# The prologue of a fused cross-attention kernel: x loaded before the context, queries in two 64-row halves, first keys written by ScalarE and VectorE

## The reference

```python
C_q  = layernorm(x) @ Wq_d                     # 512 -> 64
C_kv = ctx @ Wkv_d                             # 1601 rows, 512 -> 32
q    = (C_q @ W_qk).reshape(b, n, 16, 32)      # 16 heads
scores = einsum('bnhl,bkl->bhnk', q, C_kv) / sqrt(32)
x = x + einsum(softmax(scores), (C_kv @ Wv_u)) # by head
x = x + attention(layernorm(x), k_cache, v_cache, ...)
x = x + ffn(layernorm(x), w1, w2, w3, ...)
```

## Time and profile before

| | |
|---|---|
| Median of 3 runs | 947.01 us (943.29 to 948.63) |
| The profiled execution, its own time | 948.39 us |
| Its span in the trace | 946.6 us |
| TensorE busy | 889.5 us (94%) |
| VectorE, ScalarE, GpSimd busy | 64%, 55%, 44% |
| Mean granted clock of TensorE | 0.976 |
| First `scores` | 61.14 us |

### The profile page before, as it was taken

One profiled execution on the slowest core, in us unless ns is written; L12 is line 12 of the kernel. 1 busy time (PEld: TensorE's weight loads), 2 busy tenths in 40 slices (PEclk: granted clock), 3 DMA queues, 4 the chain that ended last, 5 costly groups with the idle time before them and its releaser, 6 DMA issues.

```text
span 946.6 us, 15443 instructions
## 1 busy us (share of the span) xinstructions
PE 889.5 (94%) x5386; PEld 658.9 (70%) x5386; DVE 604.5 (64%) x988; ACT 516.9 (55%) x1005; POOL 416.3 (44%) x270
## 2 busy tenths in 40 slices
PE   5879999999996979999999999999999998899997
PEld 3545555555442768888888888888888887788886
DVE  3445656676651538757587574875748758868884
ACT  2356666666664546636366363663636646565551
POOL 3078877787876024323233232332323333154430
PEclk9779999999998889999999999999999999999999
DMA  9836655724560721101011010110101101635521
GB/s 340 305 148 228 255 180 208 263 62 143 168 205 3 265 79 45 45 23 45 22 44 44 22 44 22 44 44 22 44 22 44 34 1 57 210 113 197 191 100 45
DMA packets 46659, 103.72 MB, mean 110 GB/s; under 512 B 11410, under 2 KB 16530, under 8 KB 45714
## 3 DMA queue, kind: packets, MB, share of 16 engines
q1 hardware_dynamic: 46050, 102.86, 31.9%
q10 hardware_dynamic: 560, 0.21, 0.1%
HBM read 97.08 MB, written 1.05 MB: 104 GB/s over the span
## 4 chain that ended last, share of the span: by engine, by line
PE 54%; DVE 5%; ACT 2%; issue 2%; POOL 1%; DMA 1%; DVEq 0%; SPq 0%; ACTq 0%
PE psum L1309 9%; PE psum L1413 8%; PE psum L1357 8%; PE psum L1295 7%; PE psum L1324 6%; PE psum L1427 4%; PE psum L1333 3%; PE psum L1338 3%; PE psum L1342 3%; DVE neg_max L1644 1%; PE psum L1325 1%; PE psum L1334 1%; PE psum L1336 1%; DVE probs_t_low L1624 1%; DVE mixed_t_low L1670 1%
## 5 line engine op out<-in xcount | busy, mean ns | idle before, releaser
L1775 POOL TENSOR_TENSOR head_probs<-head_probs,inverse_den 128x576 f32<-128x576 f32 x128 | 146.7, 1147 | 296.2 <-DVE inverse_den L1631 296.2
L945 DVE TENSOR_REDUCE max_part<-psum 128x1 f32<-128x804 f32 x128 | 120.7, 989 | 62.6 <-PE psum L674 62.6
L844 ACT ACTIVATE probs<-psum 128x512 f32<-128x512 f32 (+1 forms) x208 | 107.8, 601 | 57.4 <-PE psum L695 49.0
L1519 ACT ACTIVATE head_probs<-psum,neg_max 128x576 f32<-128x576 f32 x128 | 94.5, 738 | 78.8 <-PE psum L1325 43.0
L550 POOL TENSOR_TENSOR prob_sums<-probs 128x1024 f32<-128x1024 f32 x48 | 114.0, 2383 | 20.9 <-ACT probs L844 11.9
L1644 DVE TENSOR_REDUCE neg_max<-psum 128x1 f32<-128x576 f32 x128 | 96.2, 754 | 38.3 <-PE psum L1309 30.0
L1309 PE MATMUL psum<-k_high,query_t_high 128*128 (+1 forms) x256 | 84.5, 330 | 5.6 <-ACT head_probs L1519 2.2
L1624 DVE TENSOR_TENSOR probs_t_low<-psum,probs_t_high 128x512 fp32r<-128x512 f32 x124 | 84.8, 684 | 6.4 <-ACT probs_t_high L1525 5.4
L695 PE MATMUL psum<-q_t,c_t 97*128 97x512 f32 (+1 forms) x208 | 74.2, 438 | 9.8 <-ACT probs L844 7.0
L1324 PE MATMUL psum<-ident,head_probs 128*128 128x128 f32 x496 | 75.9, 275 | 3.2 <-DVE mixed_t_low L1670 2.4
L674 PE MATMUL psum<-c_t,q_t 96*128 96x402 f32 x256 | 74.4, 375 | 4.7 <-DVE max_part L945 2.9
(11 more groups left out here) (217 smaller groups left out, 1938.0 us busy)
## 6 DMA issues: line engine op xcount, KB each, us to landing
ctx_t_odd<-in_ctx_dram SPq DMA_DIRECT2D x4, 3202.0 KB, 11.1
w_raw<-in_L_ffn_w_dram SPq DMA_DIRECT2D x24, 448.0 KB, 5.2
w_raw<-in_L_ffn_mean_w_dram SPq DMA_DIRECT2D x24, 448.0 KB, 6.8
ffn_raw<-in_L_ffn_w_dram SPq DMA_DIRECT2D x42, 256.0 KB, 3.8
ffn_raw<-in_L_ffn_mean_w_dram SPq DMA_DIRECT2D x42, 256.0 KB, 4.1
cache<-in_ctx_dram SPq DMA_DIRECT2D x3, 3202.0 KB, 10.7
wq_nat<-in_L_attn_wq_dram SPq DMA_DIRECT2D x32, 256.0 KB, 2.7
wo_nat<-in_L_attn_wo_dram SPq DMA_DIRECT2D x32, 256.0 KB, 2.7
```

The lines of the kernel that those rows point to most:

```text
L844: act.activation(prob_buffer(b, t)[0:rows, half * BANK:(half + 1) * BANK], psum[0:rows, n % SCORE_BANKS, :], ACT.Exp, scale=XSCALE).then_i ...
L945: dve.tensor_reduce(max_part[:, qt, pair:pair + 1], psum[:, bank:bank + 2, 0:PIECE_KEYS], AX.XY, ALU.max).then_inc(s_max, 1)
L1519: act.activation(probs[:, qt, :].rearrange("p (a k) -> p a k", a=2), psum[:, 2 * (qt % 2):2 * (qt % 2) + 2, 0:HALF], ACT.Exp, bias=neg_max ...
L1775: pool.tensor_tensor(probs[:, qt, :], probs[:, qt, :], rden[:, qt:qt + 1].to_broadcast([P, KEYS]), ALU.mult).then_inc(s["norm"], 1)
```

## The change

In its own order of events:

1. **Loads.** SyncE loads x of tile 0, then tiles 1 to 3 in one DMA, then `Wkv_d` and the contexts. `Wq_d` and `W_qk` are issued by ScalarE, each twice; the angles move to SyncE, behind context 1.
2. **Two halves.** `Wq_d` stands twice side by side, so that `latent_queries` fills all 128 rows of its bank with two copies of C_q. `W_qk` is laid out on the host with heads 0 to 7 on rows 0 to 63 and heads 8 to 15 on rows 64 to 127; `queries(j)` alternates between the two halves.
3. **Order.** The statistics and the normalisation of tiles 1 to 3 come before the low parts of queries(0) on VectorE; their turns come before `compress(0)` on TensorE; `queries(1)` comes before the loop of maxima. The rotation matrix moves behind the last maximum.
4. **Keys of batch 0.** No DMA: ScalarE writes the high rows of `c_t` straight from the bank in five pieces and copies them to the third 32 rows (`first_keys`); VectorE writes the low rows in five pieces and copies the bank to `c_parts`. GpSimd's `c_low` and the fifteen DMAs are left out for batch 0, and the counts that others wait for are one batch lower.
5. **Batch 1 in parts.** `compress(1)` is cut into five parts, one behind each of the maxima 2 to 6; `natural(1)` follows maximum 7, `queries(2)` and `(3)` maxima 8 and 11. VectorE's two placements of values move behind maxima 0 and 8.
6. **Waits.** `scores(0, 0)` waits for ScalarE's copies of the queries (now in the `sums` buffers, no longer in `probs`) and not for GpSimd's low parts.

```diff
-NATURAL_BANK = (5, 2, 7) + (5,) * (BATCH - 3)
+NATURAL_BANK = (2, 2, 7) + (5,) * (BATCH - 3)
...
-QUERY_BANK = (0, 0, 2, 0)
-QUERIES_AT = {4: 1, 7: 2, 10: 3}
+QUERY_BANK = (0, 0, 0, 2)
+QUERIES_AT = {8: 2, 11: 3}
+CONTEXT_AT = {2: (0,), 3: (1,), 4: (2,), 5: (3,), 6: (DC,)}
...
-    w_qk = core.over("w_qk", [LQ, XH, 2, LKV], F32, "prob_sums4")
-    cq_t = core.over("cq_t", [LQ, TOK], F32, "prob_sums5")
-    wq_d = core.over("wq_d", [P, DC, LQ], F32, "prob_sums5", 4 * TOK)
+    w_qk = core.over("w_qk", [2 * LQ, XH // 2, 2, LKV], F32, "prob_sums4")
+    cq_t = core.over("cq_t", [2 * LQ, TOK], F32, "prob_sums5")
+    wq_d = core.over("wq_d", [P, DC, 2, LQ], F32, "prob_sums5", 4 * TOK)
...
-        return probs[(2 * (j - 1) + odd) % 4][0:LKV, :].rearrange("p (b h n) -> p b h n", b=2, h=XH // 2)
+        return sums[(2 * (j - 1) + odd) % 4][0:LKV, :].rearrange("p (b h n) -> p b h n", b=2, h=XH // 2)
...
+    def key_pieces():
+
+        bank = COMPRESS_BANK[0]
+        for g in range(GROUPS):
+            yield slice(g * LKV, (g + 1) * LKV), bank, slice(0, MAIN), slice(g * MAIN, (g + 1) * MAIN)
+        yield slice(SHIFT, P), bank, slice(MAIN, C_WIDTH), slice(FULL * P, NCTX)
...
-                if b > 0:
-                    place_part(sp, b, 2 * LKV, c_high)
-                sp.wait_ge(s_clo, b + 1)
+                place_part(sp, b, 2 * LKV, c_high)
+                sp.wait_ge(s_clo, b)
                 place_part(sp, b, LKV, c_low)
...
-            load_x(0)
-            sp.dma_start(wq_d[:, :, :], arg["Wq_d"].rearrange("(c p) q -> p c q", p=P)).then_inc(s_wq, 16)
-            qk = arg["W_qk"].rearrange("q (h l) -> q h l", h=XH)
-            for r in range(2):
-                sp.dma_start(w_qk[:, :, r, :], qk).then_inc(s_wq, 16)
+            sp.dma_start(core.x[:, 0, :], x[0:P, :]).then_inc(s_in[0], 16)
+            sp.dma_start(core.x[:, 1:TT, :], x[P:TOK, :].rearrange("(j p) e -> p j e", p=P)).then_inc(s_in[1], 16)
             sp.dma_start(w["wkv_d"][:, :, :], arg["Wkv_d"].rearrange("(c p) l -> p c l", p=P)).then_inc(s_wkv, 16)
             load_first_context(core, ctx_t, sp, s_ctx0)
-            for j in range(1, TT):
-                load_x(j)
             load_context(core, ctx_t, sp, 1, 1)
-            place_keys(0)
+            for col, angle in ((cos_col, arg["cos"]), (sin_col, arg["sin"])):
+                for odd in range(2):
+                    sp.dma_start(col[odd:P:2, 0:1], angle.rearrange("a i -> i a")).then_inc(s_rot, 16)
...
-            compressed_low(0)
-            compressed_low(1)
-            pool.wait_ge(s_clo, 2)
             for j in range(1, TT):
+                if j == 2:
+                    pool.wait_ge(s_qlo[1], 2)
+                    compressed_low(1)
+                    pool.wait_ge(s_clo, 1)
...
+                if b == 1:
+                    pe.wait_ge(s_cnat, 1)
...
-                if i == 0:
-                    pe.wait_ge(s_ct, 16 * C_COPIES * (b + 1))
+                if i == 0 and b == 0:
+                    pe.wait_ge(s_kl, GROUPS + 1)
+                    pe.wait_ge(s_kt, 1)
+                elif i == 0:
+                    pe.wait_ge(s_ct, 16 * C_COPIES * b)
...
-                    pe.wait_ge(s_cnat, 1)
+                    pe.wait_ge(s_cp, 1)
...
-                pe.wait_ge(s_wq, 3 * 16)
+                pe.wait_ge(s_wq, 4 * 16)
                 for c in range(DC):
-                    mm = pe.matmul(psum[0:LQ, LATENT_BANK[k], 0:(b - a) * P], wq_d[:, c, :], xn_t[:, c, a * P:b * P],
+                    mm = pe.matmul(psum[:, LATENT_BANK[k], 0:(b - a) * P],
+                                   wq_d[:, c, :, :], xn_t[:, c, a * P:b * P],
...
                 elif j == 2:
+                    pe.wait_ge(s_qraw, 1)
+                elif j == 3:
                     pe.wait_ge(s_cp, 2)
                     pe.wait_ge(s_cnat, 2)
-                elif j == 3:
-                    pe.wait_ge(s_qraw, 1)
-                for h in range(0, XH, 2):
-                    mm = pe.matmul(psum[:, QUERY_BANK[j] + h // 8, (h // 2 % 4) * P:(h // 2 % 4 + 1) * P],
-                                   w_qk[:, h:h + 2, :, :], cq_t[:, j * P:(j + 1) * P], start=True, stop=True)
+                for h in range(0, XH // 2, 2):
+                    for r in range(2):
+                        rows = slice(r * LQ, (r + 1) * LQ)
+                        mm = pe.matmul(psum[:, QUERY_BANK[j] + r, h // 2 * P:(h // 2 + 1) * P],
+                                       w_qk[rows, h:h + 2, :, :], cq_t[rows, j * P:(j + 1) * P], start=True, stop=True)
                 mm.then_inc(s_q, 1)
...
-            compress(0)
-            natural(0)
             for j in range(1, TT):
                 norm.tile_turn(pe, j)
+            compress(0)
             latent_queries(1)
+            natural(0)
+            queries(1)
             for i in range(MAXIMA):
                 max_scores(0, i)
-                if i == 1:
-                    compress(1)
-                if i == 3:
+                if i in CONTEXT_AT:
+                    compress(1, CONTEXT_AT[i])
+                if i == 7:
                     natural(1)
                 if i in QUERIES_AT:
                     queries(QUERIES_AT[i])
             turn_max(0)
...
-            pe.wait_ge(s_qlo[1], 2 * (TT - 1))
+            pe.wait_ge(s_qraw, TT - 1)
...
+            def first_keys():
+
+                act.wait_ge(s_c, 1)
+                act.activation(c_high[:, :], psum[:, COMPRESS_BANK[0], 0:C_WIDTH], ACT.Copy).then_inc(s_chi, 1)
+                for rows, bank, cols, keys in key_pieces():
+                    act.activation(c_t[0:LKV, 0, keys], psum[rows, bank, cols], ACT.Copy).then_inc(s_kh, 1)
+                act.wait_ge(s_kh, GROUPS + 1)
+                act.activation(c_t[2 * LKV:SHIFT, 0, 0:NCTX], c_t[0:LKV, 0, 0:NCTX], ACT.Copy).then_inc(s_kt, 1)
+
+            qk = arg["W_qk"].rearrange("q (h l) -> q h l", l=LKV)
+            for n in range(2):
+                act.dma_start(wq_d[:, :, n, :], arg["Wq_d"].rearrange("(c p) q -> p c q", p=P)).then_inc(s_wq, 16)
+            for n in range(2):
+                act.dma_start(w_qk[:, :, n, :], qk).then_inc(s_wq, 16)
             norm.tile_root(act, 0)
             norm.tile_exact(act, 0)
+            norm.rest_root(act)
             latent_copied(0)
             queries_high(0)
-            compressed(0)
-            compressed_high(0)
-            act.wait_ge(s_chi, 1)
-            place_part(act, 0, 2 * LKV, c_high)
-            norm.rest_root(act)
             for j in range(1, TT):
                 norm.tile_exact(act, j)
+            first_keys()
             latent_copied(1)
+            queries_high(1)
+            queries_copied(1)
             act.wait_ge(s_rest, 1)
             act.activation(warm[:, :], ones[:, 0:1], ACT.Exp)
             compressed(1)
             compressed_high(1)
-            for j in range(1, TT):
+            for j in range(2, TT):
                 queries_high(j)
                 queries_copied(j)
             shift_row(0)
...
+            dve.wait_ge(s_in[1], 16)
+            norm.rest_variance(dve)
+            norm.rest_normalise(dve)
             for odd in range(2):
                 dve.wait_ge(s_qhi, odd + 1)
                 dve.tensor_tensor(query_rows(0, odd, 2 * LKV, SHIFT), query_bank(0, odd, LKV),
                                   query_rows(0, odd, 0, LKV), ALU.subtract).then_inc(s_qlo[0], 1)
-            rope_matrix()
-            for j in range(1, TT):
-                dve.wait_ge(s_in[j], 16)
-            norm.rest_variance(dve)
-            norm.rest_normalise(dve)
-            place_values(0)
+            dve.wait_ge(s_chi, 1)
+            for n, (rows, bank, cols, keys) in enumerate(key_pieces()):
+                dve.wait_ge(s_kh, n + 1 if n < GROUPS - 1 else GROUPS + 1)
+                dve.tensor_tensor(c_t[LKV:2 * LKV, 0, keys], psum[rows, bank, cols], c_high[rows, cols],
+                                  ALU.subtract).then_inc(s_kl, 1)
+            dve.wait_ge(s_kl, GROUPS + 1)
+            dve.wait_ge(s_kh, GROUPS + 1)
+            dve.tensor_copy(c_parts[:, :], psum[:, COMPRESS_BANK[0], 0:C_WIDTH]).then_inc(s_cp, 1)
             for i in range(MAXIMA):
                 take_max(0, i)
-                if i == 3:
+                if i == 0:
+                    place_values(0)
+                if i == 8:
                     place_values(1)
+            dve.wait_ge(s_rest, 2)
             negate_max(0)
+            rope_matrix()
...
+def queries_by_half(a):
+    return a.reshape(LQ, 2, XH // 2 * LKV).transpose(1, 0, 2).reshape(2 * LQ, XH // 2 * LKV)
```

More of the change, by code:

```diff
@@ L390, in cross_attention @@
     warm = core.sb("exp_table_warm", [P, 1], ctx=own)
-    s_in = [core.sem(f"x_in{j}", own) for j in range(TT)]
+    s_in = [core.sem(f"x_in{j}", own) for j in range(2)]
     s_ctx0 = [core.sem(f"ctx_first_in{c}", own) for c in range(DC)]
@@ L417, in cross_attention @@
     s_ct = core.sem("c_stack_placed", own)
+    s_kh = core.sem("first_keys_high_done", own)
```

(8 more changed lines are left out.)

47 lines of the change are left out of this document (22 added, 25 removed).

## The result

The changed kernel takes 954.24 us (median of 7 runs, 949.79 to 955.57); the kernel before, run beside it, 948.63. One of its seven runs took 4,390 us; without it the median is 947.8, and the ratio, which leaves it out, is 1.007, with a 95% interval of 1.0043 to 1.0096. I had put 940.1 with a range to 947.5: slower where I said faster. The profiled execution took 954.24 us, its span is 952.4 against 946.6.

What follows compares the result with a forecast made beforehand. The prologue before the first scores, where no engine is full, was taken as the bound. First max_scores 5.85 us earlier and a 1.2 us wait saved put scores 6.9 earlier: 941.5 profiled, stated as 940.1, range 934 to 947.5.

Steps and rivals of the forecast that it cites:

- Loads: Start of the prologue: x and weights share the DMA engines, weights in by 10 us, copy of cq ends near 12.9.
- Rival A: Weights on ScalarE's queue starve behind context 0 (landing 17.3, 947 us) or context 1 too (8 more, 955); chance 0.12.
- Tile 0: Prologue, first tile: latent queries 2.2 us, queries(0) 2.8, later queries 1.5 each; queries(0) ends at 15.7.
- x before the context: Prologue: normed tiles 1 to 3 ready at 12 to 14, so TensorE's 5.06 us of idling go.
- Keys of batch 0 by the engines: After compress(0): engine copies replace fifteen hidden DMAs, c_parts at 25.85; first max_scores at 28.2 against 34.05, 5.85 us earlier.
- The loop of maxima: The sixteen maxima, with compress(1) in parts: 21.6 us against 21.5 before, worth nothing net.
- End of the prologue: Turn 2.02 and shift 1.02 unchanged, no wait for GpSimd's low parts saves 1.2; scores at 54.2 instead of 61.14.
- At nothing: Items claimed hidden at no cost: GpSimd's low parts, RoPE (1.5 us) behind the last maximum, batch 1 keys, angle loads.
- the sum: Whole kernel: 948.39 − 6.9 = 941.5 us for the profiled execution, stated as 940.1 for the median.
- B: Rival: the low clock reaches the loop of maxima, making it 5 us slower, so 945 us; chance 0.13.
- C: Rival: more gain than said, the clock stays up over the turn and batch 0, 936 us; chance 0.18.
- D: Rival: batch 0 takes the gain, by late keys of batch 1 or by GpSimd, 946 us; chance 0.05.

Runs made afterwards that it cites:

- S: The changed kernel with its four weight loads moved from ScalarE's to SyncE's queue, behind x and ahead of wkv_d and the context; 939.96 us, ratio 0.9932.
- ones late: S with GpSimd's memset of the row of ones waiting until c_parts of batch 0 is copied; 937.81 us.

## Why the prediction was wrong

**The failed step** is "Loads": "I take the weights at 10". Rival A happened, in its worse form: "Behind context 1 too, 8 more: 955", measured 954.24. It had a chance of 0.12, a third of it past 22. The copy of cq ended at 28.37, not at 12.9: 15.5 late. In the profiled span I forecast −6.9 and got +5.8, a miss of 12.7: `scores(0,0)` 14.3 later than forecast (68.51 against 54.2, as the rest of the prologue won 1.2 back), 1.8 more lost up to the negated maxima of batch 1, where RoPE stood, 3.4 given back past 280 us.

The row that could have told me was the earlier trace rows, and I used it to argue by time and size: "context 0 has smaller packets and is issued after the first weights". The question to ask of it is a count. Four loads in runs of 256 and 128 bytes make 3,072 packets; the 512 packets of context 0 let about as many through; context 1 has some 128 more, for each of which one goes. How many get through beside x and before the context the count doesn't say (it was 1,308 by 8 us), but it would have had to be over 2,400 for none to be left. So the rest must wait for the end of both contexts, and rival A's own 17.3 and 8 put that at 25.3; it was 25.98. I counted the bytes (3.7 us of the DMA engines), and alone they do go that fast. I also took it that a second issuer costs nothing on the DMA engines and only saves issue time; the kernel before with its weights on ScalarE's queue, 2.1% slower, shows that it can cost.

**Part by part**, read in S, where the weights were in time:

- *Tile 0.* Latent queries 2.05 (2.2 forecast), queries(0) 2.08 (2.8), the later ones 1.16 (1.5). The time of a sixteen was mis-sized by a quarter; it lies near the lower bounds (1.9 and 1.0), not in the middle.
- *x before the context.* No idle time before the turns, as said, but I had its cause wrong. In the kernel before, the statistics of tiles 1 to 3 began at 18.41 right behind RoPE, without a wait for x, and L175 ended at 21.32. The root came at 24.19, because ScalarE was issuing five of the key DMAs:

```profile
20.05 3.45 ACTq L469 DMA_DIRECT2D c_t<-c_high  x4
...
23.53 0.61 ACTq L471 DMA_DIRECT2D c_t<-c_high  x1
...
24.19 0.20 ACT L179 ACTIVATE norm_rstd<-norm_rstd 128x3 f32<-128x3 f32 x1 [4.17 <-issue]
```

  So 2.9 of the 5.06 us idle belong to those issues, and the fifteen key DMAs did not cost nothing. The kernel before with its weights on ScalarE's queue bears it out: x was long in, and 4.41 us of idle time stayed. The change took away the issues and the late statistics together with the late x, so no run tells what x first is worth alone.
  The normed tiles were ready at 14.2 only, at the end of my 12 to 14, because L175 was stretched; that cost 1.1 us at the copy of cq, shown by "ones late".
- *Keys of batch 0 by the engines.* ScalarE and VectorE need 4.2 us from the end of compress(0) to c_parts, as forecast (25.5 against 25.85); first `max_scores` at 27.35, forecast 28.2. Five pieces of 32 partitions took 2.10 and 2.45 us, the doubling 1.54.
- *The loop of maxima.* From the first maximum 21.4 us in S, 21.3 in the changed kernel; forecast 21.6, for either order.
- *End of the prologue.* Turn 2.02, shift 1.02, no wait for GpSimd: `scores(0,0)` 52.99 in S, forecast 54.2. Right, with 1.2 to spare from the queries and the keys.
- *At nothing.* GpSimd's low parts and the keys of batch 1 were hidden, as said. **RoPE was not**: "behind the last maximum, where VectorE waits anyway". It waits there, but so does GpSimd work there, and 1.25 us became 8.0. It cost batch 0 2.4 us in S.
- S itself: 939.96 us, ratio 0.9932. Applied to the 947.0 of the prediction that is 940.6, against 940.1 forecast. So the sum held once the weights were in time, in part by luck: 1.2 us more won in the prologue, 1.8 lost where RoPE stands, 0.6 won behind it.

**The other rivals.** B: the four large parts of compress took 0.85 to 1.51 us and the tail 0.66, so one or two of the five were slow, yet the loop was no longer than forecast; it did not decide. C: the turn took 2.02 in most runs, 1.1 in two and 1.31 in one; the clock as such gave nothing that can be counted on. D: keys of batch 1 and GpSimd were in time.

## What to carry to other kernels

Before a small load is moved to another queue, count packets, not bytes: against a queue of long packets it got one packet for each here, whatever its size; so lay it out in long rows, or put it on the same queue ahead of them. Before a short VectorE step on SBUF is moved "where the engine waits anyway", look at what GpSimd does in that stretch. Count what an engine's DMA issues hold up behind them in its own order. An edit whose cover is taken away by another edit of the same change (here the keys by DMA) has to be priced with that cover gone.

## What the runs showed of the hardware that I had not expected

- While a context was loading, the two DMA queues began packets one for one, 523 against 523 and 424 against 424, with 128 bytes on one side and 6.4 KB on the other; a queue alone began 1,418 such short packets in 1 us.
- ScalarE's issue of two small loads took 10.64 us behind some 2,590 packets that had not begun, and held up ScalarE's own work.
- Some VectorE steps on SBUF that met a running GpSimd instruction ended just behind it: 0.17 us became 3.93 (128x3), and 0.29 became 2.37 (128x128). Statistics (1.88 for three tiles), a reduction (0.17) and a step on 128x1 (0.20) on SBUF were not touched, nor were maxima over PSUM.
- Sixteen float32 passes in alternate 64-row halves take 1.16 us, one half after the other 1.71.
